# A GNN layer pair and a two-expert feed-forward layer: the feed-forward's first product taken over two chunks of nodes at once, its second product in quarters between

## The reference, cut to what matters

```python
logits = jnp.mean(x, axis=1) @ Wr + br
routing_weights = jax.nn.softmax(logits, axis=-1)
...
top_w, top_i = jax.lax.top_k(rw_tok, K)          # K = 2
top_w = jax.nn.softmax(top_w, axis=-1)
h = jax.nn.gelu(jnp.einsum('nd,edf->enf', xf, W1) + b1[:, None, :], approximate=False)
y = jnp.einsum('enf,efd->end', h, W2) + b2[:, None, :]
out = jnp.einsum('ne,end->nd', w_dense, y).reshape(B, S, D)
out = _layer_norm(out + x, gamma, beta)
```

## Time and profile before

| | |
|---|---|
| time, median of 3 runs | 2799.32 us (2798.51 to 2800.11) |
| time of the profiled execution | 2798.56 us |
| its span in the profile | 2796.8 us |
| PE busy | 2659.6 us (95%) |
| DVE, ACT, POOL busy | 2446.3 us (87%), 1875.4 us (67%), 1928.0 us (69%) |
| the feed-forward's first matmul to the end of the span | 2500.94 to 2796.8 us |

### The profile page before, as it was taken

One profiled execution on the slowest core, in us unless ns is written; L12 is line 12 of the kernel. 1 busy time (PEld: TensorE's weight loads), 2 busy tenths in 40 slices (PEclk: granted clock), 3 DMA queues, 4 the chain that ended last, 5 costly groups with the idle time before them and its releaser, 6 DMA issues. The chain is left out here.

```text
span 2796.8 us, 56641 instructions
## 1 busy us (share of the span) xinstructions
PE 2659.6 (95%) x20688; PEld 2513.3 (90%) x20688; DVE 2446.3 (87%) x4506; ACT 1875.4 (67%) x3179; POOL 1928.0 (69%) x2129
## 2 busy tenths in 40 slices
PE   4999999999999998889999999999999988969998
PEld 3999999999999998889999999999999988969998
DVE  6899999999999998978999999999999988975665
ACT  6677766666666665776766666666666656864443
POOL 7777777777777776547777777777777767952222
PEclk9999999999999999999999999999999999989999
DMA  7533333333333333443333333333333334541222
GB/s 240 179 106 106 106 106 106 106 106 106 106 106 106 106 106 102 133 156 105 106 106 106 106 106 106 106 106 106 106 106 106 106 106 134 160 134 57 68 69 68
DMA packets 162469, 312.66 MB, mean 112 GB/s; under 512 B 34061, under 2 KB 95309, under 8 KB 162229
## 3 DMA queue, kind: packets, MB, share of 16 engines
q0 software_dynamic: 79872, 218.21, 26.8%
q1 hardware_dynamic: 81120, 89.89, 9.9%
q10 hardware_dynamic: 1237, 1.41, 0.2%
HBM read 263.90 MB, written 45.48 MB: 111 GB/s over the span
## 5 line engine op out<-in xcount | busy, mean ns | idle before, releaser
L740 PE MATMUL edge_rg<-edge_rel_hi,edge_hot 128*128 128x256 f32 x6656 | 1505.7, 289 | 32.6 <-DVE edge_m_hi L707 12.4
L740 PE MATMUL edge_rg<-edge_rel_lo,edge_hot 128*128 128x256 f32 x4992 | 1271.0, 283 | 0.0
L740 PEld LDWEIGHTS edge_rg<-edge_rel_hi,edge_hot 128*128 128x128 f32 x6656 | 1186.1, 192 | 91.2 <-DVE edge_hot L605 59.4
L740 PEld LDWEIGHTS edge_rg<-edge_rel_lo,edge_hot 128*128 128x128 f32 x4992 | 957.7, 192 | 0.0
L542 ACT CAST edge_m_hi<-edge_rg 128x1024 fp32r<-128x1024 f32 x416 | 422.9, 1016 | 485.2 <-DVE edge_rg L618 485.1
L549 ACT ACTIVATE edge_hot<-edge_typ,minus_type 128x512 fp32r<-128x512 f32 x832 | 527.0, 685 | 168.2 <-PE edge_typ L723 164.7
L605 DVE TENSOR_SCALAR edge_hot<-edge_typ,type_of 128x512 fp32r<-128x512 f32 x832 | 582.8, 743 | 12.5 <-ACT edge_hot L549 8.9
L624 DVE TENSOR_TENSOR edge_m_lo<-edge_rg,edge_m_hi 128x1024 fp32r<-128x1024 f32 x416 | 509.6, 1225 | 87.5 <-ACT edge_m_hi L542 80.8
L531 POOL DMA_INDIRECT work<-h,src x416 | 394.0, 947 | 137.2 <-issue 107.5
L531 POOL DMA_INDIRECT work<-emb,src x416 | 394.5, 948 | 131.2 <-issue 108.1
L531 POOL DMA_INDIRECT edge_xg<-emb,src x416 | 393.5, 946 | 129.7 <-issue 112.7
(11 more groups left out here) (183 smaller groups left out, 3929.0 us busy)
## 6 DMA issues: line engine op xcount, KB each, us to landing
work<-emb,src POOLq DMA_INDIRECT x416, 2.8
edge_xg<-emb,src POOLq DMA_INDIRECT x416
work<-h,src POOLq DMA_INDIRECT x416, 2.8
edge_xg<-h,src POOLq DMA_INDIRECT x416
set_x_rows<-in_x SPq DMA_DIRECT2D x25, 256.0 KB, 3.9
emb<-set_e_rows SPq DMA_DIRECT2D x25, 256.0 KB, 2.9
emb_t<-acc SPq DMA_DIRECT2D x5, 1280.0 KB, 15.7
dense_prev<-emb_t SPq DMA_DIRECT2D x25, 256.0 KB, 2.8
```

The source lines that it names most:

```text
L740: ins = pe.matmul(rg[q % 2][:, t, :], hot[:, q % 2, c, t * P:(t + 1) * P], part[:, c, :], start=(c == 0 and part is rel_hi), stop=(c == FULL))
```

## The change

Chunks are taken in pairs (`SPANS` = 13 of them, the last with chunk 24 alone); below, "span" with a number or `m` means such a pair. `widen(m, u)` runs each unit's six matmuls over both chunks, 512 moving columns, so `up` is filled bank by bank. The second product is cut in four quarters of two units (`STEPS_UP` = 4), and PE's program becomes: quarter q of `narrow` of pair m - 1, then two units of `widen` of pair m, four times over. One such round of four is called turn m below. `full` is a ring of two quarters, `hid` holds one pair (8 units x 512). `down` has two buffers of two banks, and the routing product's bank is one of them. Queues of SP and POOL keep their text: they still go chunk by chunk. The loops are written out instead of repeated by the engines' loop instruction.

```diff
-        full = carve(2, U // 2, CHUNK, part=work)
-        hid = [s.sb(f"hid{k}", [P, 2, U, CHUNK], F32R) for k in range(2)]
+        full = work[:, used:used + 2 * STEP * SPAN].rearrange("p (r u n) -> p r u n", r=2, u=STEP)
+        hid = [s.sb(f"hid{k}", [P, U, SPAN], F32R) for k in range(2)]
...
-        down = [s.ps(f"down{k}", [P, 2, DIM]) for k in range(2)]
-        route = s.ps("route", [P, 512])
+        down = [[s.ps(f"down{k}{h}", [P, 2, DIM]) for h in range(2)] for k in range(2)]
+        route = down[1][1][:].rearrange("p j d -> p (j d)")
...
             def moments(c, b, n):
-                dve.wait_ge(down_done, c + 1)
+                dve.wait_ge(down_done, c // 2 + 1)
                 dve.wait_ge(biased, 2 * c + 2)
...
-            over_chunks(dve, (2, moments), (0, low(0)), (2, finish), (0, low(1)), (0, w2_low))
+            for m in range(SPANS + 2):
+                ready = chunks_of(m - 2) if m > 1 else []
+                for q in range(STEPS_UP):
+                    if q < len(ready):
+                        moments(ready[q], ready[q] % 2, ready[q] // 2)
+                    if m < SPANS:
+                        low(m, q)
+                    if 0 <= q - 1 < len(ready):
+                        finish(ready[q - 1], ready[q - 1] % 2, ready[q - 1] // 2)
+                    if m == 0 and q == 1:
+                        dve.wait_ge(w2_split, 1)
+                        dve.tensor_tensor(w2[1], w2_raw, w2[0].bitcast(F32), ALU.subtract).then_inc(w2_split, 1)
...
+            def widen(m, u):
+
+                if m == 0 and u % STEP == 0:
+                    pe.wait_ge(w1_lo, u // STEP + 1)
+                wait_past(pe, gelu_done, U * m + u - 3)
+                out = up[u % 4][:, 0:wide(m)]
+                nodes = slice(2 * m, 2 * m + 2) if len(chunks_of(m)) == 2 else slice(2 * m, 2 * m + 1)
+                each = wide(m) // len(chunks_of(m))
+                out = out.rearrange("p (o n) -> p o n", n=each)
+                for k in range(DC):
+                    ins = product(pe, out, [w[:, u // HC, k, (u % HC) * P:(u % HC + 1) * P] for w in w1],
+                                  [K["ln_parts"][:, part, nodes, k, 0:each] for part in range(2)],
+                                  k == 0, k == DC - 1)
+                ins.then_inc(up_done, 1)
+
+            def narrow(m, q):
+
+                pe.wait_ge(hid_lo, STEPS_UP * m + q + 1)
+                if q == 0:
+                    wait_past(pe, y_done, 2 * (m - 1))
+                    if m == 0:
+                        pe.wait_ge(w2_split, 2)
+                for u in units(q):
+                    for h, j in blocks_of(m):
+                        at = slice((2 * h + j) * P, (2 * h + j + 1) * P)
+                        a, b = [v[:, u, at] for v in hid], [w[:, u // HC, u % HC] for w in w2]
+                        out = down[m % 2][h][:, j, :]
+                        for k, (x, z) in enumerate(((1, 0), (0, 1), (0, 0))):
+                            ins = pe.matmul(out, a[x], b[z], start=(u == 0 and j == 0 and k == 0),
+                                            stop=(u == U - 1 and k == 2), skip_group_check=True)
+                if q == STEPS_UP - 1:
+                    ins.then_inc(down_done, 1)
+
+            for m in range(SPANS + 1):
+                for q in range(STEPS_UP):
+                    if m > 0:
+                        narrow(m - 1, q)
+                    if m < SPANS:
+                        for u in units(q):
+                            widen(m, u)
...
+            for m in range(SPANS):
+                for q in range(STEPS_UP):
+                    gelu(m, q)
+                    high(m, q)
+                    if m == 0 and q == 1:
+                        act.wait_ge(weighted, 2)
+                        act.copy(w2[0], w2_raw).then_inc(w2_split, 1)
```

More of the change, by code:

```diff
@@ L1259, in phase_ffn @@
         U = TOP * HC
+        STEP = 2
+        STEPS_UP = U // STEP
+        SPAN = 2 * CHUNK
+        SPANS = -(-CHUNKS // 2)
         area = K["in_deg"][:]
@@ L1340, in phase_ffn, with chunks_of, blocks_of, wide @@
         act_passed = s.sem("act_passed")
+        def chunks_of(m):
+            return [c for c in (2 * m, 2 * m + 1) if c < CHUNKS]
+        def blocks_of(m):
+            return [(h, j) for h, c in enumerate(chunks_of(m)) for j in range(parts(c))]
+        def wide(m):
+            return P * len(blocks_of(m))
+        def units(q):
+            return range(STEP * q, STEP * (q + 1))
         block = ctx.enter_context(nc.Block())
@@ L1447, in _, with low @@
                                      ALU.add).then_inc(weighted, 1)
[L1449 to L1463, removed]
+            def low(m, q):
+                dve.wait_ge(hid_hi, STEPS_UP * m + q + 1)
+                at, to = slice(STEP * q, STEP * (q + 1)), slice(0, wide(m))
+                dve.tensor_tensor(hid[1][:, at, to], full[:, q % 2, :, to], hid[0][:, at, to].bitcast(F32),
+                                  ALU.subtract).then_inc(hid_lo, 1)
             def moments(c, b, n):
-                dve.wait_ge(down_done, c + 1)
+                dve.wait_ge(down_done, c // 2 + 1)
                 dve.wait_ge(biased, 2 * c + 2)
                 at = slice(0, parts(c))
-                dve.tensor_tensor(y[:, b, at], down[b][:, at], xl[:, b, at], ALU.add).then_inc(y_done, 1)
+                dve.tensor_tensor(y[:, b, at], down[c // 2 % 2][b][:, at], xl[:, b, at], ALU.add).then_inc(y_done, 1)
                 dve.wait_ge(y_done, c + 1)
@@ L1500, in _ @@
             ins.then_inc(logits_done, 1)
[L1502 to L1527, removed]
@@ L1529, in _ @@
-            over_chunks(pe, (0, widen), (1, narrow))
+            def widen(m, u):
[11 more added lines that the diff above has]
+                ins.then_inc(up_done, 1)
@@ L1544, in _ @@
             act.wait_ge(b1_in, 16 * TOP)
[L1546 to L1576, removed]
+            def gelu(m, q):
+                wait_past(act, hid_lo, STEPS_UP * m + q - 1)
+                if m == 0 and q < 2:
+                    act.wait_ge(w1_lo, 2 * q + 2)
+                for v, u in enumerate(units(q)):
+                    act.wait_ge(up_done, U * m + u + 1)
+                    act.activation(full[:, q % 2, v, 0:wide(m)], up[u % 4][:, 0:wide(m)], ACT.Gelu,
+                                   bias=b1_sb[:, u // HC, u % HC:u % HC + 1]).then_inc(gelu_done, 1)
@@ new lines, in high @@
+            def high(m, q):
+                act.wait_ge(gelu_done, U * m + STEP * (q + 1))
+                at, to = slice(STEP * q, STEP * (q + 1)), slice(0, wide(m))
+                act.copy(hid[0][:, at, to], full[:, q % 2, :, to]).then_inc(hid_hi, 1)
+            for m in range(SPANS):
[5 more added lines that the diff above has]
+                        act.copy(w2[0], w2_raw).then_inc(w2_split, 1)
```

## The result

| | before | after |
|---|---|---|
| time, median of 10 runs each | 2801.21 us (2798.51 to 2803.78) | 2806.61 us (2804.93 to 2810.03) |
| ratio | | 1.0021, 95% interval 1.0013 to 1.0029 |
| span of the profiled execution | 2796.8 us | 2804.4 us |

The changed kernel is slower by 5.4 us in the medians, 0.2%, and by 7.6 us between the two profiled executions. Seven more runs of the kernel before lifted its median by 1.9 us over the three that were shown first.

A forecast was written before the change was run, and what follows sets the result against it. PE was taken as the bound from the phase's first matmul on. Terms -6.9 + 0 + 0 + 10.7 = +3.8 us on the span of 2796.8; forecast 2802.5 us, own range 2799 to 2805.5, 8 in 10 2795.5 to 2808.

The forecast's parts named there:

- fourth rival: PE's 2.2 us gap lets the clock fall (+1.5) and changes of output cost +2.1: 2806 us; chance 0.08.
- Term 4: Tail behind PE's end: bias and load still go chunk by chunk; 20.2 us where 9.5 stood, +10.7 us.
- Term 1: First product behind `narrow(0)`: 528 wide matmuls at 226.5 ns instead of two narrow ones at 239.6, -6.9 us.
- Term 3: Second product in quarters: output changes every 3 matmuls rather than every 24, +2.1 us at most, taken as 0.
- Term 2: Phase start, pair 0: wide matmuls save nothing, PE idles 2.2 us for W2's low part, ready as before; 0 us.
- columns alone count: Wide matmuls take 213.3 ns, a longer matmul hiding the weight load: -13.9 instead of -6.9, 2795.5 us; chance 0.10.
- the overlap: Wide matmuls overlap one another, each paying only the 111.5 ns weight-load floor: -67.6 instead of -6.9, 2741.8 us; chance 0.01.
- a wide matmul saves nothing: Moving columns fetched from two chunks cost the 13 ns again: 2809.4 us; chance 0.08.
- the tail does not grow: Loads 22 and 24 and their biases get out before they are wanted, the 10.7 drop out: 2791.8 us; chance 0.07.

The follow-up runs named there:

- Experiment two: Changed kernel with four instead of two buffers for the residual rows, loads waiting four chunks back, POOL's bias two chunks ahead of its deviation: ratio 0.9994 to the kernel before.
- experiment five: Changed kernel with `finish(22)` ahead of `moments(23)` on DVE in the last whole pair's turn only: ratio 1.0021 to the kernel before.
- experiment three: Changed kernel with block loop outside, unit loop inside a quarter, so the second product's output changes every 6 matmuls instead of 3: ratio 1.0021 to the kernel before.
- experiment seven: Changed kernel with every second unit, the one ahead of the second product, in two pieces of 256 columns: ratio 1.0028 to the kernel before.
- the first experiment: Changed kernel with each unit's first product in two pieces of 256 moving columns again, all else as changed: ratio 1.0035 to the kernel before.
- experiment four: Changed kernel with PE's turn in halves: two quarters of the second product, then four units of the first, twice: ratio 1.0024 to the kernel before.
- the sixth: Changed kernel with pairs ending at chunk 21 and chunks 22 to 24 done one by one, two row buffers kept: ratio 1.0007 to the kernel before.

## Why the prediction was right, point by point

The predicted 2802.5 us was 0.1% above the median shown, 2799.32. Measured is 2806.61: inside the range for 8 in 10, 2795.5 to 2808, but above the forecast's own 2799 to 2805.5 and above the 2804.9 up to which the prediction counted no change; it had given that outcome 0.20. 1.9 us of the 4.1 us of error are the median before, which seven more runs put at 2801.21. Against that median the change costs 5.4 us, 0.2%, where 3.2 were forecast over the median shown; the difference of the two spans, 7.6 us, was forecast as 3.8. The direction and its reason, a tail that costs more than PE gains, were right. That the number comes nearest to the fourth rival's 2806 is luck, as told below.

**Term 4, the tail (+10.7, measured +10.1), was right in its mechanism and its size.** With T at 2765.2 (PE's end less 19.6) the prediction puts `moments(22)` at 2784.6, `moments(23)` at 2790.1, `finish(22)`'s end at 2794.1; the trace has 2784.58, 2790.06 and 2793.94. Only the last load landed 0.4 us sooner than I had. Experiment two takes the waits away and 7.3 us with them; experiment five shows that one link, the load behind `finish(22)`, was not worth its own length.

**Term 1, the wide matmul (-6.9, measured -5.1), was mis-sized.** "Adding 256 columns to today's: 119.8 + 106.7 = 226.5 ns" holds in pair 0 once its distances have settled (226.7) but not behind a second product, where a burst of wide matmuls costs 40 ns more whether it has 12 or 24; in quarters that is 230 ns each. By 528 x (239.6 - 230) it is 5.1 us. The Trainium skill ("TensorE: Matmul & The Clock Gate", "Back-to-back issue gap") has a formula for an isolated matmul that gives 215.8 ns, and a figure of about 131 ns for a stream of loads and matmuls. The changed kernel's trace agrees with neither: 226.7 ns at best, 230 in mid-phase. The 14 neighbours at 0.22 us in the prediction were rounding: in the unrounded starts of the whole trace before, no successor of that 512-column matmul stands nearer than 227 ns.

**Term 3, the second product (0, measured +1.9), was wrong in its value and its bound's cause.** "I take 0, the wait being the likelier cause." The distance rose from 118.8 to 120.4 ns on 1176 matmuls. The bound of +2.1 had the right size by chance: experiment three halves the changes of output and nothing moves, experiment seven puts narrow matmuls between and the distance is back at 118.3. Terms 1 and 3 together are the 3.8 us by which PE's stretch missed the forecast (268.4 for 264.6). With the higher median before, they are why the time lies high in the range.

**Term 2, pair 0 (0, measured -0.8 counted from the first matmul).** The stall came, released by the low part of W2 as said, but shorter, for two reasons that the term did not have: the warm-up lasted ten wide matmuls, and the low part ran faster without POOL beside it (2.28 us; 3.37 before, when POOL's bias ran beside its first 1.2 us). The 1.4 us by which the phase began later is not explained by the change: 1.1 of it lies ahead of the phase, in code that is the same, and 0.2 in the landing of W1's first part.

Of the rivals, "columns alone count" and the overlap are refuted by 226.7, "a wide matmul saves nothing" by the first experiment, "the tail does not grow" by the trace. The fourth, gap and changes of output, got near its 2 us for a reason it did not name, and its clock fall did not come.

What stays open is why the second product runs at 120.4 ns behind a 512-column matmul and at 118.3 behind a 256-column one. In the unrounded starts its distances repeat 117, 120, 123 ns in the first case and go through 115 to 122 in the second; behind the 128-column matmuls of turn 12 the 115s are back. The weight loads take 0.19 us in both, and the granted clock is 1.00 in both.

## What to carry to other kernels

Widening a tile on the engine that bounds the middle also widens what is left when that engine stops: price the last tile's whole chain, each link with the queue it stands in, before counting the gain per matmul. When two units come free at once, every helper that still goes one by one (a load that waits for a finish, a bias behind a reciprocal) becomes serial; buffers that were deep enough for one are not for two. And the best version here was not the change or its undoing but the change with the cover restored: the rows' ring deeper, the last chunks single, PE's turn in halves; it is 0.14 to 0.17% faster than the kernel before.

## What the runs showed of the hardware that was not expected

- A matmul of 256 columns with its weight load starts every 118.3 to 118.8 ns in one order and every 120.2 to 120.4 in another; 512-column matmuls right ahead of it are enough to move it, through 48 matmuls at least (5.77 us in experiment four).
- A burst of 12 or 24 512-column matmuls behind 256-column ones takes 226.7 ns each and 40 ns once, most of it in the first eight distances; the six of experiment seven take 28 ns more than six times 226.7. Distances of 228 to 236 ns also stand in pair 0 right behind the rise of the clock, so the 256-column neighbours need not be the cause.
- Two DVE instructions on 128x256 (the first step of `finish`) take 0.73 us alone and 2.61 to 2.63 us while POOL adds on 128x512; DVE's low part of W2 took 3.37 us beside POOL and 2.28 behind it. In the tail this swallowed the gain of experiment five, and in the sixth it became a wait of PE.
